# Attention with gating: the product of state and gate moves from GpSimd to VectorE

## What is computed

```python
def _time_mix_layer(x, ln_w, ln_b, Wk, Wv, Wr, Wo):
    normed = _layer_norm(x, ln_w, ln_b)
    k = jnp.einsum('btd,ed->bte', normed, Wk)
    v = jnp.einsum('btd,ed->bte', normed, Wv)
    r = jax.nn.sigmoid(jnp.einsum('btd,ed->bte', normed, Wr))
    kv = k * v
    def step(state, kv_t):
        state = DECAY * state + (1.0 - DECAY) * kv_t
        return (state, state)
    _, states = jax.lax.scan(step, init, jnp.swapaxes(kv, 0, 1))
    y = r * jnp.swapaxes(states, 0, 1)
    y = jnp.einsum('btd,ed->bte', y, Wo)
    return x + y
```

## Time and profile before

| what | value |
|---|---|
| median of 3 runs | 1263.43 us (1262.25 to 1264.12) |
| the profiled execution | 1267.21 us, its span 1265.4 us |
| busy over the span | PE 87%, DVE 73%, POOL 68%, ACT 52% |
| product on POOL (line 298) | 62 times, 80.2 us in all, 1293 ns each |
| POOL idle before the products | 70.7 us, 67.0 of them until DVE's recurrence |

### The profile page before, as it was taken

One profiled execution on the slowest core, in us unless ns is written; L12 is line 12 of the kernel. 1 busy time (PEld: TensorE's weight loads), 2 busy tenths in 40 slices (PEclk: granted clock), 3 DMA queues, 4 the chain that ended last, 5 costly groups with the idle time before them and its releaser, 6 DMA issues. The chain is left out here.

```text
span 1265.4 us, 23767 instructions
## 1 busy us (share of the span) xinstructions
PE 1103.8 (87%) x7172; PEld 988.0 (78%) x7172; DVE 926.9 (73%) x1973; ACT 656.5 (52%) x1091; POOL 858.0 (68%) x696
## 2 busy tenths in 40 slices
PE   6899888988888889748999999999999999999910
PEld 5778777777777777636888888888889999999910
DVE  5678888888888887745776666666667888888737
ACT  4455555555455554324554454444555666566618
POOL 3355777777777777666666776666677676777634
PEclk9899999999999999859999999999999999999965
DMA  4011111111111111157656666656668898998559
GB/s 150 17 51 58 48 48 51 51 50 50 50 50 50 50 51 34 34 129 185 160 139 147 161 158 154 143 137 157 151 157 224 238 237 227 238 246 229 134 167 381
DMA packets 80662, 164.20 MB, mean 130 GB/s; under 512 B 27424, under 2 KB 45600, under 8 KB 80352
## 3 DMA queue, kind: packets, MB, share of 16 engines
q1 hardware_dynamic: 49248, 126.16, 31.8%
q0 software_dynamic: 31360, 37.38, 15.7%
HBM read 118.01 MB, written 45.49 MB: 129 GB/s over the span
## 5 line engine op out<-in xcount | busy, mean ns | idle before, releaser
L1163 POOL DMA_INDIRECT x_acc<-fy_sb,pair_out x142 | 284.7, 2005 | 152.9 <-DVE fy_sb L1264 76.9
L1319 PE MATMUL fring<-fxh,fw_hi 128*128 128x256 f32 (+1 forms) x816 | 265.3, 325 | 4.0 <-DVE fxl L1255 1.9
L1321 PE MATMUL fring<-fxh,fw_lo 128*128 128x256 f32 (+1 forms) x816 | 265.3, 325 | 0.0
L1320 PE MATMUL fring<-fxl,fw_hi 128*128 128x256 f32 (+1 forms) x816 | 265.0, 325 | 0.0
L1182 ACT ACTIVATE fw_hi<-w_raw 128x1024 fp32r<-128x1024 f32 x153 | 161.1, 1054 | 149.0 <-PE fy L1362 132.4
L1235 DVE TENSOR_TENSOR fw_lo<-w_raw,fw_hi 128x1024 fp32r<-128x1024 f32 x153 | 186.5, 1219 | 17.8 <-ACT fw_hi L1182 16.5
L88 POOL DMA_INDIRECT xg<-x_src,pair_in x142 | 159.8, 1125 | 43.3 <-issue 42.7
L78 POOL DMA_INDIRECT slot_list<-pairs,slot_u x128 | 140.1, 1095 | 47.6 <-issue 30.9
L1319 PEld LDWEIGHTS fring<-fxh,fw_hi 128*128 128x128 f32 x816 | 153.7, 188 | 18.0 <-issue 4.1
L1360 PE MATMUL fy<-fw_hi,gh 128*128 128x256 f32 x568 | 163.7, 288 | 0.9 <-issue 0.9
L1321 PEld LDWEIGHTS fring<-fxh,fw_lo 128*128 128x128 f32 x816 | 153.8, 189 | 13.3
(11 more groups left out here) (148 smaller groups left out, 2378.8 us busy)
## 6 DMA issues: line engine op xcount, KB each, us to landing
w_raw<-w_ffn SPq DMA_DIRECT2D x153, 512.0 KB
x_in<-h SPq DMA_DIRECT2D x16, 512.0 KB, 3.3
x_src<-x SPq DMA_DIRECT2D x16, 512.0 KB
x_acc<-x SPq DMA_DIRECT2D x16, 512.0 KB
acc<-x_acc SPq DMA_DIRECT2D x16, 512.0 KB, 7.7
out<-o SPq DMA_DIRECT2D x16, 512.0 KB, 6.8
xg<-x_src,pair_in POOLq DMA_INDIRECT x142
x_acc<-fy_sb,pair_out POOLq DMA_INDIRECT x142
```

Of the source, the lines that this page charges most:

```text
L1163: nc.gpsimd.indirect_dma_start(x_acc, bass.IndirectOffsetOnAxis(pair_out[j][:, q, 0:1].bitcast(U32), 0), y[j][:, q, :], None, compute_op=A ...
L1319: nc.tensor.matmul(out, hi, rows_hi, start=dc == 0, stop=False)
L1320: nc.tensor.matmul(out, hi, rows_lo, start=False, stop=False)
L1321: last = nc.tensor.matmul(out, lo, rows_hi, start=False, stop=dc == DC - 1)
```

## The change

The calls of `gated` leave POOL's list and go to DVE's. On DVE, in a step with both layers:

- layer 1, e = 0: directly behind `recur(0, s, 0)`
- layer 1, e = 1: behind `x_lo(1, s - 1)`
- layer 2, e = 0: behind `x_lo(0, s + 1)`, ahead of `place`
- layer 2, e = 1: directly behind `recur(1, s - 1, 1)`, last in the step

`y_lo`, `rstd` and the scatters stay on POOL. Nothing else is changed.

```diff
--- before.py
+++ after.py
@@ -582,11 +582,8 @@
                     scatter_pairs(nc, kept, slot_list, j, 0, Q)
                     gather_rows(nc, pool, kept, x_src, s_met, 0, 0, Q)
                 scatter(s, j, 0, 2)
-                if layer1:
-                    gated(pool, 0, s, 0)
                 scatter(s, j, 2, 2)
                 if layer1:
-                    gated(pool, 0, s, 1)
                     y_lo(pool, 0, s, 0)
                 if within(s, 1, CHUNKS - 2):
                     rstd(0, s + 1)
@@ -596,14 +593,11 @@
                 if within(s, 2, CHUNKS + 1):
                     rstd(2, s - 2)
                 scatter(s, j, 5, 1)
-                if layer2:
-                    gated(pool, 1, s - 1, 0)
                 scatter(s, j, 6, 1)
                 if layer2:
                     y_lo(pool, 1, s - 1, 0)
                 scatter(s, j, 7, 1)
                 if layer2:
-                    gated(pool, 1, s - 1, 1)
                     y_lo(pool, 1, s - 1, 1)
 
             run(pool, step)
@@ -777,14 +771,19 @@
                 if at(s, CHUNKS):
                     residual2(s, j)
                 if layer1:
-                    for e in range(DC):
-                        recur(0, s, e, j)
+                    recur(0, s, 0, j)
+                    gated(dve, 0, s, 0)
+                    recur(0, s, 1, j)
+                    if not layer2:
+                        gated(dve, 0, s, 1)
                 if at(s, 0):
                     x_lo(0, 1)
                     keep_bias(1)
                     low_weights(1)
                 if layer2:
                     x_lo(1, s - 1)
+                    if layer1:
+                        gated(dve, 0, s, 1)
                 if within(s, 1, CHUNKS - 2):
                     dve.wait_ge(s_x[1 - j], half * 16 + 16 * (1 + j))
                     norm_stats(0, x_in[:, 1 - j, :, :], s + 1)
@@ -804,6 +803,8 @@
                     recur(1, s - 1, 0, j)
                 if within(s, 1, CHUNKS - 2):
                     x_lo(0, s + 1)
+                if layer2 and not at(s, CHUNKS):
+                    gated(dve, 1, s - 1, 0)
                 if within(s, 3, CHUNKS + 2):
                     place(s - 3, half, j)
                 if at(s, EARLY + 2):
@@ -811,6 +812,7 @@
                     big_table(nc, dve, kept)
                 if layer2 and not at(s, CHUNKS):
                     recur(1, s - 1, 1, j)
+                    gated(dve, 1, s - 1, 1)
 
             run(dve, step)
             dve.wait_ge(s_base, CHUNKS + 1)
```

## The result

The changed kernel takes 1270.95 us (1269.56 to 1272.77, 4 runs), the kernel before 1263.56 in the same session (1262.25 to 1264.12, 4 runs). The ratio is 1.0056, with a 95% interval of 1.004 to 1.0071: slower by 0.6%, where 1275 was forecast. The profiled execution took 1270.02 us, with a span of 1268.2.

The account below looks back on a forecast made before the run. One ring per step, mostly on DVE, was taken as the bound. Eight loop steps at 1.25 (10.0), plus 0.8, plus 1.5, less 0.5 gave 11.8 us; 1263.4 + 11.8 = 1275 us, range 1255 to 1280.

Parts of the forecast that it names:

- lead: How far the recorded start of DVE's layer 1, e = 1 product is ahead of POOL's `yl`; read as 0.69 us.
- The recurrence: Layer 1, e = 1 on DVE: without POOL's product beside it, 2.21 becomes 1.28 us, mean gain 1.0 a step.
- The first contest: DVE's layer 1, e = 1 product against POOL's `yl`: if lost, `g` 0.35 us late; if won, 1.0 early.
- steps 4, 5 and 14: Written-out steps with scatters: 0.35 - 0.61 + 0.5 = 0.25 us slower each, 0.8 together, with `slot_u` winning.
- the second contest: DVE's `slot_u` against POOL's `yl` in layer 2: if DVE loses, 0.41 us cost; if it wins, 0.61 gain.
- the rival in which DVE wins both: Product and `slot_u` both start ahead of `yl`: -1.1 us in eleven steps, 1252 us; chance 0.13.
- `ve` gives back, `z` a little late: Behind layer 1's shut-out product, statistics 1.5 us late, `ve` returns 1.12, `z` and `g` 0.35 late in the mean.
- Layer 2, e = 0: Product ahead of `slot`: `slot_u` shut out by `yl`, next `kv` at X + 3.94 instead of X + 3.53, cost 0.41 us.
- X: Start of the DVE `xl` that stands ahead of layer 2's e = 0 product; 308.09 in step 9 before.
- Layer 2, e = 1: Product open at the step's end, 0.62 us; every second step's loop-branch idle of 0.44 may hide it; mean 0.5.
- Steps 1 to 3: Steps without scatters: two open products (1.2 us) less what collisions give back, 0.5 each, 1.5 together.
- Step 15: Step 15 and the way out of the attention phase: a gain of about 0.5 us.

Follow-up runs that it names:

- first_only: Kernel before with only the product of layer 1, e = 0 moved to DVE, behind its recurrence in the stall for `k_sb`: 1252.2 us, ratio 0.9912.
- after_no_loop: Changed kernel with the eight loop steps written out: 1250.97 us, ratio 0.9888; its control, the kernel before written out, 0.9949.
- all_but_second: Changed kernel with the product of layer 1, e = 1 back on POOL: 1261.9 us, ratio 0.9977.
- low_half_later: Changed kernel with POOL's `yl` of layer 1, e = 0 put behind the next chunk's reciprocal deviations: 1270.51 us, ratio 1.004.
- second_ahead: Changed kernel with the product of layer 1, e = 1 directly behind its recurrence, ahead of layer 2's `xl`: 1272.37 us, ratio 1.0057.
- pool_delay: Changed kernel with a spare memset of 128 x 128 on POOL between the third and fourth scatter: 1261.21 us, ratio 0.9963.
- second_only: Kernel before with only the product of layer 1, e = 1 moved to DVE, behind layer 2's `xl`: 1270.46 us, ratio 1.0055.
- vector_delay_256: Changed kernel written out, with a spare memset of 128 x 256 on DVE ahead of the product of layer 1, e = 1: 1248.54 us, ratio 0.9855.
- two_no_loop: Kernel before written out, with the products of e = 0 of both layers on DVE, those of e = 1 on POOL: 1246.88 us, ratio 0.9879.

## Why the prediction was right, and where it was off

The direction, the time to 4 us and the mechanism in the loop held; the rest of the sum was wrong in both directions. There is luck in it twice. Errors of opposite sign stand beside each other in the sum, which gave 11.8 where the medians differ by 7.4. And the loop's contest was called lost at a lead of 0.69, where the runs show that 0.69 wins. By the prediction's own terms the lead is 0.67 (293.73 + 0.81 + 1.28 is 295.82, not 295.84), which lies between the leads that lost and 0.68, where it went both ways. The contest was lost because the lead turned out as 0.57 to 0.65. The reason given, that POOL gets its way from the moment it stands in line, was right; the place of the edge was not known.

**The recurrence** was forecast at 1.28 and is. `first_only` shows what it is worth alone: 12 us of the kernel.

**The first contest** was forecast lost, by 0.36 + 0.16 against 0.43, with a product of 2.4 us. In the eight loop steps it is lost with 2.42 to 2.51. In steps 4, 5 and 14 it is won. The failing step is the sentence "there `slot_u` is less held up by loop registers": the loop's register work was applied to the second contest alone. The loop shifts the first by 0.12 as well, and that was all it took; which of its instructions does it, no run shows. Those three steps were put at +0.25 each; they are -1.6, -1.3 and -1.1, the price of the rival in which DVE wins both (-1.1). Shown by `after_no_loop`, in which the loop steps win as well.

**`ve` gives back, `z` a little late**: from the `kv` behind the stall to `g` it was 11.90 in the earlier trace rows and is 12.32, +0.42 where 0.35 was put as a mean.

**Layer 2, e = 0**: `yl` was put at X + 2.70 and stands there (315.56 - 312.86), the next `kv` at X + 3.94 and is at X + 3.90. The difference of 0.03 that decided the second contest came out as 0.02, on the side forecast. A number like that could have gone the other way.

**Layer 2, e = 1**: from that `kv` to the next `u` it was 6.39 (318.01 - 311.62) and is 6.60 (323.36 - 316.76), +0.21 in the step whose idle the product can hide. In the other kind of step the whole difference is 1.21 instead of 1.01. Together a loop step is +1.17, forecast 1.25.

**Steps 1 to 3** were put at 1.5 and cost 4.3. The estimate let collisions give 0.5 back in each. In steps 1 and 2 they took instead: the product of layer 2, e = 1, the one forecast as merely open, meets the `yl` of e = 0 there and takes 1.52 and 1.42. Step 1, DVE and then POOL:

```profile
61.09 1.28 DVE L686 TENSOR_TENSOR_SCAN state<-decay,carry,kv 128x512 f32<-128x512 f32 x1
...
62.48 1.52 DVE L298 TENSOR_TENSOR y<-state,r_sb 128x512 f32<-128x512 f32 x1
```

```profile
61.20 2.25 POOL L305 TENSOR_TENSOR yl<-y,yh 128x512 fp32r<-128x512 f32 x1 [6.46 <-ACT yh L409]
```

The low half is first held by the recurrence, and then holds the product until 64.00. Step 3 costs 1.5 (30.57 against 29.05) without such a collision: the product takes 0.69, and the two open ones cost their 1.3 with nothing given back. That layer 2's products cause it is shown by `first_only`, whose steps 1 to 3 are as before (26.41, 27.30, 29.03), and `all_but_second`, whose are not.

**Step 15** was put at -0.5 and is -3.3. I read it so, and no run shows it: in the last step with both layers nothing stands behind layer 2's output product to fill PE, so the chain from recurrence to `yl` counts in full. From the end of the last recurrence to the end of `yl` it was 4.15 (506.86 to 511.01) and is 2.96 (514.23 to 517.19). This and the recurrence, 1.58 instead of 2.35, are 2 of the 3.3; the rest wasn't followed. `all_but_second` has the gain (36.85), `first_only` not (40.18).

So 11.8 was the sum and 5.7 the measure: the loop right (10.0 against 9.4), the start 2.8 too low, steps 4, 5 and 14 4.8 too high, the end and the stretch ahead of step 1 some 3.5 too high.

**The cause.** The theory was that the product loses its place to a `yl` that stands in line behind a scatter. The rival was DVE's load: three open products of 0.62 in a step. The rival is right for a part: with the product of layer 1, e = 1 on POOL, the two products of layer 2 still add 0.7 to a loop step (32.4 in `all_but_second`, 31.75 in `first_only`), though `slot_u` is shut out in both. The 33.0 of `low_half_later` and `second_ahead` isn't a measure of load alone, since the norm or `xl` is late there, and where the contest is won in `pool_delay` the step is 32.6 in the mean. Load can't explain `pool_delay`, nor the alternation in `second_only`, nor that the changed kernel gains once the loop is gone. That the product's length in the loop goes by the moment of POOL's operation is shown. What fixes that moment, and when DVE's own place is taken, is not: `vector_delay_256` doesn't fit a rule of recorded starts.

## What to carry to other kernels

Look for the one moved instruction that falls into a stall and move that alone: here it was worth 12 us, and the three others together cost some 18 (1.0056 against 0.9912). Where two engines shut each other out, compare the order in which both stand in line, not only their durations, and do it apart for looped and written-out steps, since a tenth of a microsecond of loop work can turn a collision in every round. An edit that takes a collision away at one place should be followed to the place where the delayed operation runs next: `low_half_later` and `two_no_loop` fell short of their expectation for that reason.

## What the runs showed of the hardware

A POOL operation queued behind an indirect DMA can win against an operation of DVE that has the earlier recorded start. Over all kernels with this pair, product on DVE directly behind `xl` against `yl` behind the fourth scatter, leads of 0.57 to 0.65 us always lost and leads of 0.69 and more always won; at 0.68 it went both ways. At that edge (0.68 to 0.70) the scatter had been running for 0.29 to 0.32 us when the product started. The Trainium skill (SBUF — State Buffer, section "Who interferes with whom") says that issue order decides who blocks. The traces agree only if issue isn't the recorded start: the recorded start of POOL's operation stands some 0.68 us further behind the moment that counts than that of the product does. Whether all of it lies on POOL's side is open, by `vector_delay_256`.

The scatter itself gives way to a recurrence that runs already, which reads two SBUF operands: 1.96 us instead of 0.96 at 296.89, ending 0.78 after it. In the attention phase of every trace a scatter held in this way ends 0.75 to 0.82 after the recurrence. A scatter that started ahead of the recurrence was not held. The same section infers that a `tensor_tensor` doesn't hold up the writing of descriptors. The traces agree for the product: in step 4 it runs from 136.46 to 137.14, wholly inside a scatter that takes 0.96. For the recurrence, another operation, they show the hold.

In the loop, an instruction of DVE that depends on the one ahead of it starts about 0.1 us later than written out (0.89 against 0.79 from `kv` to the recurrence, 296.79 - 295.90 and 133.88 - 133.09), and the kernel before is 0.5% faster without its loop.
